# Who issues the first groups' loads, and in which order the first slots of an edge pipeline run

## The reference, cut to what matters

```
h = relu(layernorm(x))
edge_feat = concat(h[src], h[dst], edge_attr)        # 512 + 512 + 64
m = mish(mish(edge_feat @ W1 + b1) @ W2 + b2)
agg = segment_sum(m, dst)
u = mish(concat(h, agg) @ W3 + b3);  x1 = x + layernorm(h + u @ W4 + b4) * gamma + beta
```

## Time and profile before

| | us |
|---|---|
| median of 3 runs | 1547.55 (1547.35 to 1548.13) |
| the profiled execution | 1548.88 |
| its span | 1547.2 |
| PE busy in it | 1502.3 (97%) |
| DVE, ACT, POOL busy | 1418.2, 1297.7, 1080.3 |

### The profile page before, as it was taken

How to read it: one execution, slowest core, us unless ns; L and a number is a source line. 1 busy time by engine, 2 the same in 40 slices (tenths; PEclk the granted TensorE clock), 3 DMA queues, 4 the chain that set the end, 5 groups by cost and what they waited for, 6 DMA issues and landing times.

```text
span 1547.2 us, 33384 instructions
## 1 busy us (share of the span) xinstructions
PE 1502.3 (97%) x7862; PEld 1172.1 (76%) x7862; DVE 1418.2 (92%) x2922; ACT 1297.7 (84%) x2505; POOL 1080.3 (70%) x984
## 2 busy tenths in 40 slices
PE   7869999999999999999999999999999999999998
PEld 5657777777777777777777777777777777776785
DVE  7579999999999999999999999999999999995666
ACT  4049999999999999999999999999999999986352
POOL 1236878888878788887888887888887887752220
PEclk9979999999999999999999999999999999999999
DMA  8854555555555555554555555554554555544663
GB/s 275 322 181 107 125 123 116 124 123 116 124 123 116 122 124 116 122 124 114 125 121 115 126 117 117 127 119 116 127 117 117 128 118 117 135 107 125 136 144 152
DMA packets 122451, 205.09 MB, mean 133 GB/s; under 512 B 31641, under 2 KB 54297, under 8 KB 122416
## 3 DMA queue, kind: packets, MB, share of 16 engines
q0 software_dynamic: 59392, 116.85, 35.1%
q1 hardware_dynamic: 63024, 87.83, 18.7%
HBM read 151.60 MB, written 42.75 MB: 126 GB/s over the span
## 4 chain that ended last, share of the span: by engine, by line
PE 79%; issue 5%; DVE 5%; POOL 4%; DMA 3%; ACT 1%; POOLq 1%; SPq 0%; DVEq 0%; ACTq 0%
PE bm L1069 47%; PE bp L1048 6%; PE bp L1056 5%; PE bs L1092 4%; PE bp L1058 4%; PE pm L1080 2%; PE po L2008 2%; PE pu L1986 2%; PE pA L678 1%; DMA xg<-A_tab,idx 1%; PE pm L1079 1%; PE pu L335 1%; POOL hTl L975 1%; PE pB L678 1%; POOL M_tab L1000 1%
## 5 line engine op out<-in xcount | busy, mean ns | idle before, releaser
L975 POOL TENSOR_TENSOR hTl<-tp,hTh 128x512 fp32r<-128x512 f32 (+1 forms) x314 | 411.2, 1309 | 231.4 <-DVE khl L1251 203.4
L1069 PE MATMUL bm<-W2h,hTh 128*128 128x512 f32 x1252 | 498.3, 398 | 2.9 <-POOL hTl L975 2.3
L1069 PE MATMUL bm<-W2l,hTh 128*128 128x512 f32 x1252 | 497.2, 397 | 0.0
L1069 PE MATMUL bm<-W2h,hTl 128*128 128x512 f32 x1252 | 494.6, 395 | 0.0
L964 POOL DMA_INDIRECT xg<-A_tab,idx x305 | 319.2, 1047 | 49.8 <-issue 37.0
L1069 PEld LDWEIGHTS bm<-W2h,hTh 128*128 128x128 f32 x1252 | 235.5, 188 | 72.9 <-DVE bm L1244 15.1
L1129 ACT ACTIVATE rp<-bp 128x512 f32<-128x512 f32 (+1 forms) x314 | 183.8, 585 | 120.3 <-PE bp L1058 118.9
L1069 PEld LDWEIGHTS bm<-W2l,hTh 128*128 128x128 f32 x1252 | 235.5, 188 | 57.5
L1069 PEld LDWEIGHTS bm<-W2h,hTl 128*128 128x128 f32 x1252 | 235.6, 188 | 53.4
L1215 DVE SCALAR_TENSOR_TENSOR rp<-rp 128x512 f32<-128x512 f32 (+1 forms) x314 | 215.3, 686 | 34.6 <-ACT rp L1129 22.3
L1225 DVE SCALAR_TENSOR_TENSOR tp<-rp,bp 128x512 f32<-128x512 f32 (+1 forms) x314 | 211.4, 673 | 3.2 <-ACT rp L1135 0.8
(11 more groups left out here) (244 smaller groups left out, 2327.7 us busy)
## 6 DMA issues: line engine op xcount, KB each, us to landing
ea<-in_eaT SPq DMA_DIRECT2D x156, 128.0 KB
M_tab<-mev POOLq DMA_DIRECT2D x157, 80.0 KB
agg_tab<-ev POOLq DMA_DIRECT2D x157, 64.0 KB
db<-in_dst_rows SPq DMA_DIRECT2D x78, 128.0 KB
M<-M SPq DMA_DIRECT2D x78, 128.0 KB
eaW<-Bh_tab SPq DMA_DIRECT2D x79, 64.0 KB
eaW<-Bl_tab SPq DMA_DIRECT2D x79, 64.0 KB
xg<-A_tab,idx POOLq DMA_INDIRECT x313
```

The source lines that it names most:

```text
L975: e.tensor_tensor(hTl[p][:, j, 0:w], pick(u, start_t, tp)[:, 0:w], hTh[p][:, j, 0:w], ALU.subtract)\
L1069: last = e.matmul(bank[0:r, :], a[p][:, c, j * P:j * P + r], w[:, c, :], start=False, stop=c == KC - 1 and w is W2l, skip_group_check=True)
```

## The change

SP gives up the copies and B rows of groups 0 and 1; ACT issues them, at the head of its edge program, with the same waits. SP goes straight to the loads of group 2 (`At(None, 8)`), then two of the late zeros, then the loads of group 3 (`At(None, 12)`), then the other two zeros, which no longer wait for `s_pre` themselves; the loop starts at 2 and not at 1. On POOL, slot -2 has no gather and slot -1 has two (`ts = (0, 1)`), so that low(3) comes before both. On DVE, `prep(8, 0)` moves from before slot 0 into slot 0, behind `pre(4, 1)`.

```diff
+        def rows(e, p, b):
+            e.dma_start(eaW1[p][0:32, :].bitcast(F32), Bh_d[bass.ds(b, WIN), :]).then_inc(q_win[p], 16)
+            e.dma_start(eaW1[p][32:64, :].bitcast(F32), Bl_d[bass.ds(b, WIN), :]).then_inc(q_win[p], 16)
+        def copy(e, p, n):
+            e.dma_start(M1[p][64:128, 0:n].bitcast(F32), M2[p][64:128, 0:n].bitcast(F32)).then_inc(q_win[p], 16)
...
         @work.on("sync")
-            b = [e.value_load(base_i[0:1, 3 * g:3 * g + 1], min_val=0, max_val=NP - WIN) for g in range(2)]
-            e.wait_ge(s_prep, 1)
-            copy(0, G)
-            e.wait_ge(s_prep, 3)
-            copy(1, G)
-            b_stored(e)
-            rows(0, b[0])
-            rows(1, b[1])
-            for i, n in zip(range(M_EARLY, NCH), (1, 2, 2, 3)):
-                e.wait_ge(s_pre, n)
+            loads(At(None, 8))
+            for i in range(M_EARLY, M_EARLY + 2):
                 zero_m(e, i, q_zlate)
-            with e.Fori(1, FULL // 2) as i:
+            loads(At(None, 12))
+            for i in range(M_EARLY + 2, NCH):
+                zero_m(e, i, q_zlate)
+            with e.Fori(2, FULL // 2) as i:
                 loads(At(i, 0))
                 loads(At(i, 4))
...
         @work.on("gpsimd"), step(s)
+                    if s.reg is None and s.const in (-2, -1):
+                        ts = (0, 1) if s.const == -1 else ()
...
         @work.on("scalar"), ahead of the first pre_chain
+            b = [e.value_load(base_i[0:1, 3 * g:3 * g + 1], min_val=0, max_val=NP - WIN) for g in range(2)]
+            e.wait_ge(s_prep, 1)
+            copy(e, 0, G)
+            e.wait_ge(s_prep, 3)
+            copy(e, 1, G)
+            b_stored(e)
+            rows(e, 0, b[0])
+            rows(e, 1, b[1])
...
         @work.on("vector"), step(s), behind pre(u, 1)
+                if s.reg is None and s.const == 0:
+                    prep(At(None, 2 * SUB), 0)
...
-            prep(At(None, 2 * SUB), 0)
             slots(e, 0, LOOP0, LOOP1, LAST, step)
```

More of the change, by code:

```diff
@@ L920, in loads @@
                 wait(e, s_pre, u.val(1, -4))
-                rows(p, b)
+                rows(e, p, b)
                 e.wait_ge(s_prep, u.group(2, 1))
[L923 to L930, removed]
-            b = [e.value_load(base_i[0:1, 3 * g:3 * g + 1], min_val=0, max_val=NP - WIN) for g in range(2)]
-            e.wait_ge(s_prep, 1)
-            copy(0, G)
-            e.wait_ge(s_prep, 3)
-            copy(1, G)
-            b_stored(e)
-            rows(0, b[0])
-            rows(1, b[1])
-            for i, n in zip(range(M_EARLY, NCH), (1, 2, 2, 3)):
-                e.wait_ge(s_pre, n)
+                copy(e, p, n)
+            loads(At(None, 8))
+            for i in range(M_EARLY, M_EARLY + 2):
                 zero_m(e, i, q_zlate)
-            with e.Fori(1, FULL // 2) as i:
+            loads(At(None, 12))
+            for i in range(M_EARLY + 2, NCH):
+                zero_m(e, i, q_zlate)
+            with e.Fori(2, FULL // 2) as i:
                 loads(At(i, 0))
```

## The result

| | before | after |
|---|---|---|
| median of 20 runs each | 1547.5 (1544.69 to 1550.36) | 1551.17 (1549.16 to 1553.14) |
| ratio | | 1.0023 (1.0017 to 1.0029) |
| span of the profiled execution | 1547.2 | 1548.2 |

The change makes the kernel 3.6 us slower, by the ratio, and the time lies outside the predicted range. The two profiled spans differ by 1.0 us only. For 1.2 us of the rest the reason lies ahead of the change: in the execution profiled after, the last store of B is issued at 82.16 us and not at 83.36. Another 1.4 us lies behind the start: from PE's slot 4 to the end of the span it is 1427.95 us before and 1426.52 after, and why was not followed up.

What follows compares the result with a forecast made beforehand. PE's own work was taken to bound the kernel from about 115 us, leaving only its start to win. Gains of 1.2, 1.6 and 0 less 1.3 made 1.5 us, from 1547.55 to 1546.0 us, range 1543.6 to 1548.4.

Steps and rivals of the forecast that it cites:

- Term 3: SP's order at the start: indices no longer late, the moved zeros through before the fourth gather's data moves; costed at nothing.
- rival 4: Slower: two zeros behind group 2's copy delay the last gather and the clock falls; 1550.1 us, chance 0.08.
- Term 1: First B rows, issued by ACT instead of SP, start earlier: 1.2 us gained, range -0.8 to 1.7.
- the rule quoted in the prediction: Trainium skill: all issuers' DMAs share 16 engines, a second issuer saves only sequencer time; puts the rows' gain between 0.3 and 1.4.
- Term 2: POOL's and DVE's new orders let group 2's fourth gather issue 1.6 us earlier, ends 1.1 and 2.2.
- Term 4: PE waits 2.4 us for group 2's last gather and its clock falls: 1.3 us lost, ends 0 and 1.5.
- rivals: 1: No fall of PE's clock at the start, the rest as forecast: 2.8 us gained, 1544.7 us; chance 0.30.
- condition of 2: Rival: first B rows land no earlier, as ACT's issues are dear or group 2's inputs in front; 1547.3 us, chance 0.13.
- 3 is refuted: Rival: the reordering changes nothing, since low(5) waits for DVE's slot 1; only the rows' gain remains; 1546.3 us, chance 0.07.
- the signs of being wrong: PE's last start wait is another one, the gather takes over 4.5 us to land, or new PE waits at 115 to 315.

Runs made afterwards that it cites:

- z_last: The changed kernel with all four late zeros behind group 3's loads; 1548.8 us, ratio 1.0008 to the kernel before.
- z_four: The changed kernel with all four late zeros between group 2's and group 3's loads; 1552.01 us, ratio 1.0024 to the kernel before.
- sp_undone: The changed kernel with SP's zeros and group 2 loads ordered as before; ACT's rows, POOL's and DVE's new orders stay; 1546.51 us, ratio 0.9989.
- rows_act: The kernel before with only ACT issuing the copies and rows of groups 0 and 1; 1547.39 us, ratio 0.9992.
- inputs_late: As z_gap, but SP waits for s_pre of 1 before issuing group 2's idx, ea and db; 1545.21 us, ratio 0.9986.
- z_gap: The changed kernel with the four late zeros behind group 2's idx, ea and db, ahead of its rows; 1547.87 us, ratio 0.9996.
- sp_only: The kernel before with SP's new order alone, SP still issuing copies and rows of groups 0 and 1; 1549.78 us, ratio 1.0009.
- g_pairs: sp_undone with POOL issuing group 2's third and fourth gathers together behind low(4), ahead of low(5); 1546.7 us, ratio 0.9993 to the kernel before.
- g_all: sp_undone with POOL issuing all four gathers of group 2 behind low(3), ahead of low(4); 1545.8 us, ratio 0.9975 to the kernel before.

## Why the prediction was wrong

The four terms, as forecast and as the traces of the changed kernel give them:

| term | forecast | measured | from |
|---|---|---|---|
| 1, the rows by ACT | -1.2 | +0.3 | 6.87 - 6.55 |
| 2, POOL's and DVE's order | -1.6 | -1.4 | 20.19 - 21.61 |
| 3, SP's order (zeros) | 0 | +2.7 | 6.54 - 3.85 |
| 4, the clock | +1.3 | +2.0 | 5.92 - 3.88 |
| sum | -1.5 | +3.6 | |

**Term 3 is the step that failed.** I costed the two moved zeros at nothing, because at 338 GB/s their 1280 KB would be through in 3.8 us, at about 110, when the last gather's data moves. They took longer: the two landed 5.4 and 6.3 us after their issue, the second at about 111.9. I had charged the engines with the zeros alone. In the same stretch stand group 2's copy, the third gather, group 3's inputs (384 KB, of which I followed only the indices) and its rows; the trace shows the engines full from 106 to 115 us. It was my rival 4, with a chance of 0.08 and a place and price that were right in kind: it said 3.8 us of delay, it was 2.7, and gave 1550.1. z_last, with no zeros ahead of the gather, has none of the delay and z_four, with four, has more of it, so the zeros are the cause that can be named; sp_undone shows that without SP's new order the loss is gone. What share the inputs beside the zeros have in the 2.7 us, no run separates. What made the case likely was in view: the indices under four zeros took 5.43 us, and in the trace of the kernel before the zeros themselves landed 3.7 to 6.8 us after their issue.

**Term 1 had the right parts and the wrong weights.** ACT was free as early as I said: the rows' low half was issued at 85.63, which is 3.47 us behind the last store of B (88.02 - 83.36 = 4.66 before), and one row to the next took it 0.5 to 0.9 us. With SP as before this is worth 6.55 - 5.27 = 1.28 us (1.0 in rows_act). But I charged group 2's inputs in the same stretch with 0.2 us, and they cost 1.3 (inputs_late against z_gap) to 1.7 (sp_undone against z_gap), all that ACT had gained. The lower end that I gave by the rule quoted in the prediction, a gain of 0.3 with all inputs in front, was nearer than my 1.2; the measured loss of 0.3 lies outside it too, for 384 KB at 338 GB/s are 1.1 us and they cost more. The Trainium skill (DMA: Bandwidth & Descriptors, section Issuing engines are not separate DMA queues) has it that the DMAs of all issuers interleave on the same engines; the traces agree, with 3.41 us to the rows' landing beside the inputs and 2.09 without.

**Term 2 held**, 1.4 of 1.6 us, and so did its working: prep of group 2 without a wait, PE's wait for POOL down from 2.3 to 0.9 us. The forecast of no wait there over 0.5 us was missed by little. But the cause is shared: with SP's order as before POOL's and DVE's moves bring 1.2 us (21.43 to 20.22, 0.6 each), and SP's order brings 1.3 without them (20.32 in sp_only). The two do not add up. In the presence of the one, the other brings 0.13 us or less (20.32, 20.22 and 20.19).

**Term 4 held in kind.** A wait of some 2.4 us at PE was forecast for a gather that lands in 3.7 us; it was 2.22 to 2.29 in the four kernels where it did with both moves of term 2 (z_last, sp_undone, z_gap, inputs_late). The clock fell in three of these four, and in the changed kernel with its wait of 5.3. But the forecast that a wait of this length brings the fall is half right: with a wait of 2.29 us the clock fell in sp_undone (slot 3: 5.36 us) and not in g_pairs (3.88), with 2.22 in z_gap (5.41) and not in inputs_late (3.86), and it fell with 1.89 in rows_act. The price of a fall is 1.5 us, as forecast. In the changed kernel it was 2.0 and in z_four 2.6: the slow stretch was longer there, in the changed kernel from 115.8 to 120.2 us. The table takes the whole 2.0 as a loss; the fall of the kernel before, behind its wait of 2.3 us for POOL, lay ahead of the last wait and cost nothing there.

The other rivals: 1 would need an unhindered gather and no fall. The condition of 2, that the rows land no earlier, came true beside rival 4. With both, the prediction's own prices give 1547.55 - 1.6 + 3.8 + 1.5 = 1551.25 us, and 1551.17 was measured; that it is so near is luck, for the delay of the gather was 1.1 us less than priced, and rows and clock cost 0.3 and 0.5 more. The prediction prices no two rivals together. 3 is refuted by rows_act against sp_undone in the trace, 21.43 against 20.22 us. Of the signs of being wrong one came, the gather over 4.5 us to land (6.41); PE shows no new wait from 118 to 315 us.

Open: why g_pairs, whose profiled start promises 3.0 us, measured 1.1. The two profiled executions are not middling ones: the 1548.88 of the kernel before is 1.4 us above its median of 1547.5, the 1545.24 of g_pairs 1.5 below its own. Falls of the clock in executions that were not profiled fit too: of the twelve of g_pairs the three with a mean granted clock of 0.989 or 0.990 took 1548.15 to 1550.93 us, the nine with 0.991 to 0.993 took 1543.97 to 1548.14, and 3 us at half the clock lower the mean by 0.001. Where in the kernel these falls lie is not on record, so this is argued, not shown. Nor was it tried to bring inputs_late and g_all together.

## What to carry to other kernels

A transfer that nobody waits for can still have a price: here it was paid by the gather that shared its time and that the path was waiting for. Before a large fill or prefetch is moved, list everything that is in flight in its new place, in bytes and from all issuers, and divide by the rate of a full stretch, and do not take the result for the time to landing; put it where the DMA share is low and PE is in a stage that waits for no DMA. And freeing an issuer early helps only if what it issues next does not overtake the load that the path is waiting for; one wait on the consumer of that load put this right here (inputs_late).

## What the runs showed of the hardware that I had not expected

A gather issued earlier landed no earlier, or hardly, when the gathers stood closer together. Of the four of group 2 (256 KB each), the last took 3.5 us to PE's slot 3 when issued 2.9 us behind the third (sp_undone), 4.9 when 1.5 us behind it (g_pairs), and 6.0 when all four were issued within 4.2 us (g_all). From 106 to 110 us the busy share of the DMA engines was 0.92 to 1.03 in g_all, at about 250 GB/s, and 0.73 to 0.81 in g_pairs, so full engines alone do not account for both. What limits the gathers, and which part is due to group 3's inputs beside them, the runs do not say.
